# First attention of a fused two-layer kernel: the next batch's projections in two halves, small pieces of TensorE work between the score matmuls, the index load moved to the head of a batch, and the output rows placed in the values' PSUM bank

## The chip, the cores and the metric

The kernel runs on one core of one Trainium2 chip. The metric is the device time of one launch in microseconds (us), lower is better. The core has TensorE (PE, with its weight loads as PEld), VectorE (DVE), ScalarE (ACT), GpSimd (POOL) and SyncE (SP), which run at the same time and wait for each other through semaphores only, and 16 DMA engines, fed by queues of SP, ACT and POOL.

## The reference

Two transformer-like layers over x (16 batches, 128 x 256, float32), cut to what matters:

```python
def _L0_cond_ref(x, mask, Wq, Wo):          # B, D, T = 16, 128, 256; 8 heads of 16
    xt = jnp.transpose(x, (0, 2, 1))
    q = xt @ Wq.T
    qh = q.reshape(B, T, NH, dk).transpose(0, 2, 1, 3)
    scores = scale * jnp.einsum('bhqd,bhkd->bhqk', qh, qh)
    logits = (scores * cmask + (1.0 - cmask) * NEG) * rmask
    attn = jax.nn.softmax(logits, axis=-1)
    ctx = jnp.einsum('bhqk,bhkd->bhqd', attn, qh)
    ...
    out = ctx @ Wo.T
    return jnp.transpose(out, (0, 2, 1))
x = x + _L0_ffn_ref(_L0_cond_ref(x, cond, Wq, Wo), lut, gate_idx, up_idx, down_idx)
x = x + _L1_ffn_ref(_L1_cond_ref(x, cond[:, None, :], ...), ...)
```

`_L0_ffn_ref` is a gated feed-forward net whose weights are entries of a table of 16 values, picked by integer indices (`w = lut[idx]`). `_L1_cond_ref` is a second attention with 16 heads, `_L1_ffn_ref` a mixture of four experts. The change touches the first attention alone, during which the table weights of the first feed-forward net are also built.

## The kernel before, in words

Every engine has a program of its own, written out by hand; its order is the order of the code, and only semaphores (`S["..."]`) tie the engines together. The stages follow one another: the first attention (from some 24 to 298 us of the span), the first feed-forward net, the second attention, the routing, the experts.

The first attention runs over 16 batches. A `body(i, ...)` on each engine works on three of them at once: batch i gets its row maxima, batch i - 1 its softmax and contexts, batch i + 1 its projections. "Batch period" below means the time from one body's first score matmul to the next one's.

The steps of one batch b, with the lines of the profile:

- PE `project` (L764): four matmuls, one for each pair of heads (two instructions each), from the masked x `xm` into PSUM `PA`. The first two fill its first half (512 columns), the last two its second half. ACT `stacks(b, par, h)` (L521, L522) turns half h into bf16 stacks `ks` and `qs`, DVE `lows` (L1170) makes the low parts `low`, and SP `patch` (L313, L317) moves rows of `low` and of the mask into the stacks, by three small DMAs for each half (semaphores `pt0`, `pt1`): one for the mask, behind `ks`, and two of 32 rows of 1 KB behind `lows`.
- PE `scores` (L780) into the two banks of `PB`, one call for each pair c (0 to 3) and row group s (0, 1); it waits for `pt{c // 2}`. DVE `maxima` (L1178) reduces each bank to the row maxima; three short operations (L1185, L1187, L1189) put them into `mcol`, PE `max_rows` (L828) transposes them into `PD`, DVE `add_max` (L1194) adds them into `qs`.
- PE `scores_T` (L792) then makes the transposed scores with the maxima already subtracted, in the two banks of `PC`; it waits for `add_max` (`q2`). ACT `exps` (L536) takes exp of each bank into `probs`.
- PE `project_v` (L772) and ACT `values` (L528) make the values; PE `contexts` (L804) multiplies them with `probs` into `PD[:, 0:512]`, in two calls with `max_rows` of the next batch between; DVE `normalise` in four steps (L1200, L1203, L1206, L1213) divides by the sum; PE `outputs0` (L835) is the output projection; ACT `context_out` (L541) copies it out of PSUM, and POOL `context_parts` (L393, L396) splits it in two bf16 parts. POOL `projected` (L401) masks x two batches ahead.
- Beside it, one chunk c of table weights for each batch (17 chunks, so one is left after the 16 batches): ACT `load_hot` (L550) issues a load of 1 MB of indices (8 rows of 8 KB, each copied to 16 partitions), DVE `one_hot` (L1164) compares, PE `look_up` (L816) multiplies with the table into `PD[:, 512:1024]`, ACT `looked_up` (L546) copies out.

The order around the change is in the `body` functions of PE, ACT and DVE and their calls behind the loop. PE's queue, in order: for each c the calls `scores`, `scores_T` for s = 0 and 1, then a block of other work (`project_v` behind c = 0, the whole `look_up` behind c = 1, `outputs0` and two projections behind c = 2, two projections behind c = 3), then contexts, maxima, contexts. A call of `scores` waits until DVE has reduced the same bank's content from two calls before, a call of `scores_T` until ACT has taken it.

Of the kernel before, what the change touches and what calls it, by code (L numbers as in the profile page):

```python
# [14 lines left out]
P = 128  # L15
B, D, T = 16, 128, 256
# [62 lines left out]
def program(nc, x, cond, condT, consts, wqT, woT, lut, idx_all, w_emb, b_emb, g_norm, w_qkv, g_q, g_k,  # L79
            w_out, w_outT, w_r, b_r, w_all, out, tok_x, tok_r, idx_low, absent_d):  # L80
    with ExitStack() as ctx:
# [420 lines left out]
        def _(act):  # L502
# [13 lines left out]
            def stacks(b, par, h):  # L516
                o = slice(h * 512, (h + 1) * 512)
                act.wait_ge(S["pq"], 2 * b + h + 1)
                if not (isinstance(b, int) and b < 2):
                    act.wait_ge(S["st"], 8 * (b - 1))  # L520
# [17 lines left out]
            def context_out(b):  # L538
                act.wait_ge(S["wo"], b + 1)
                unless_first(act, S["cl"], b)  # L540
                nc.scalar.copy(c_out, PD[:, 512:512 + T]).then_inc(S["c"], 1)  # L541
# [15 lines left out]
            def body(i, par, before=True, after=True):  # L557
                exps(i - 1, 0)
                values(i - 1, 1 - par)
                exps(i - 1, 1)  # L560
                looked_up(i - 1)
                load_hot(i + 1, 1 - par)
                exps(i - 1, 2)
                if before:
                    context_out(i - 2)
                exps(i - 1, 3)
                if after:
                    stacks(i + 1, 1 - par, 0)
# [7 lines left out]
            body(LAST, 1, after=False)  # L576
            exps(LAST, 0)
# [173 lines left out]
        def _(pe):  # L751
# [45 lines left out]
            def contexts(b, par, s):  # L797

                pe.wait_ge(S["vu"], b + 1)
                pe.wait_ge(S["ex"], 8 * b + 8)  # L800
# [8 lines left out]
            def look_up(c, par):  # L809
                pe.wait_ge(S["onehot"], c + 1)  # L810
                pe.wait_ge(S["q2"], min(c + 1, B) if isinstance(c, int) else c + 1)
                if isinstance(c, int) and c >= B:
                    pe.wait_ge(S["c"], LAST)
                bank = PD[:, 512:1024].rearrange("p (h c) -> p h c", h=2)
                for j in range(LPC):
                    ins = mm(bank[:, :, j * LG:(j + 1) * LG], hot[:, par, j * P:(j + 1) * P],  # L816
                             lutw[:].rearrange("p h g -> p (h g)"), start=True, stop=True)
                ins.then_inc(S["lmm"], 1)

            def max_rows(b):  # L820
                pe.wait_ge(S["mc"], 3 * b + 3)
                unless_first(pe, S["w0"], b)
                if not (isinstance(b, int) and b < 2):
                    pe.wait_ge(S["c"], b - 1)
# [6 lines left out]
            def outputs0(b):  # L831
                pe.wait_ge(S["ct"], b + 1)
                pe.wait_ge(S["w0"], LCH if isinstance(b, int) and b == LAST else b + 2)
                for qt in range(KT):
                    ins = mm(PD[:, 512 + qt * P:512 + (qt + 1) * P], cT[:, qt * P:(qt + 1) * P], wo1[:], start=True, stop=True)  # L835
# [12 lines left out]
            def body(i, par, half, before=True, after=True):  # L848
                for c in range(4):
# [3 lines left out]
                    if c == 0:  # L853
                        project_v(i - 1, 1 - par, half)
                    if c == 1:
                        look_up(i - 1, 1 - par)
                    if c == 2 and before:
                        outputs0(i - 2)
                    if c >= 2 and after:
                        project(i + 1, 1 - par, 2 * c - 4)  # L860
# [773 lines left out]
```

## Time and profile before

| | |
|---|---|
| median of 3 runs | 783.81 us (780.01 to 785.44) |
| the profiled execution | 782.84 us, span 781.2 us |
| PE busy in the span | 605.0 us (77%) |
| DVE busy | 430.9 us (55%) |
| ACT busy | 322.0 us (41%) |
| POOL busy | 111.8 us (14%) |
| mean granted clock of TensorE | 0.863 |
| batch 1's first score matmul to batch 15's | 43.75 us to 277.32 us |

The time is that of the launch on the device; the span is the part of it that the profiled instructions fill, 1.6 us less. A busy share is an average over five stages with different limits, so it tells nothing of the stage in question. A granted clock of 1.00 is 2.4 GHz, one of 0.50 is 1.2 GHz; values between are stretches with both. Matmuls overlap in the array, and their ends are modelled, so a busy PE need not be a PE at its peak.

### The profile page before, as it was taken

The numbers are of one execution on the slowest core, as the hardware profiler recorded it, in microseconds if no ns is written. First come the engines' busy times: TensorE is split into PE (matmuls) and PEld (weight loads), VectorE is DVE, ScalarE is ACT, GpSimd is POOL, SyncE is SP. The second block draws the span as 40 slices with busy tenths as digits, with TensorE's granted clock in tenths as the row PEclk, the third lists the DMA queues.
The fourth block names the chain that finished last, engine by engine and source line by source line (L and its number), as shares of the span: only waits on it lengthen the run. The fifth ranks groups of instructions, "written<-read, shape, count | busy, mean of one in ns | idle before, by whom it ended". The sixth has DMA issues, their size and how long they took to land. (4 is left out here: it accounts for less than half of the span.)

```text
span 781.2 us, 15202 instructions
## 1 busy us (share of the span) xinstructions
PE 605.0 (77%) x4891; PEld 375.2 (48%) x4923; DVE 430.9 (55%) x957; ACT 322.0 (41%) x575; POOL 111.8 (14%) x145
## 2 busy tenths in 40 slices
PE   1456788867778869999956787788628999999992
PEld 1134455544455445555533454454414666666662
DVE  2455665675665664334336999999852333333331
ACT  1133454544454543233336777777502222222220
POOL 3401111111111001000000000000011333333321
PEclk9576666786666798999989999999958999999997
DMA  8863333333333320000036566555210111111110
GB/s 281 180 166 79 75 88 96 93 93 76 75 90 87 87 73 2 1 1 0 0 76 179 126 147 146 145 147 137 75 21 28 42 41 40 38 40 43 44 34 3
DMA packets 32739, 62.42 MB, mean 80 GB/s; under 512 B 7109, under 2 KB 19975, under 8 KB 30280
## 3 DMA queue, kind: packets, MB, share of 16 engines
q1 hardware_dynamic: 22112, 23.99, 10.7%
q0 software_dynamic: 6432, 18.46, 10.5%
q10 hardware_dynamic: 4168, 19.61, 9.7%
q8 instruction: 17, 0.28, 0.2%
q14 instruction: 10, 0.08, 0.0%
HBM read 58.81 MB, written 7.82 MB: 85 GB/s over the span
## 5 line engine op out<-in xcount | busy, mean ns | idle before, releaser
L1178 DVE TENSOR_REDUCE nmax<-PB 128x2 f32<-128x512 f32 x128 | 83.7, 677 | 93.8 <-PE PB L780 93.8
L536 ACT ACTIVATE probs<-PC 128x512 f32<-128x512 f32 x128 | 69.5, 595 | 132.2 <-PE PC L792 132.1
L780 PE MATMUL PB<-small 64*128 64x256 bf16 x256 | 46.6, 377 | 69.2 <-DMA small<-small 69.2
L1562 DVE TENSOR_TENSOR probs<-PC,probs 128x1024 bf16<-128x1024 f32 x19 | 23.3, 1225 | 79.9 <-ACT probs L729 65.6
L729 ACT CAST probs<-PC 128x1024 bf16<-128x1024 f32 x19 | 19.2, 1012 | 113.7 <-PE PC L1090 95.6
L764 PE MATMUL PA<-small,wq 128*128 128x256 f32 x128 | 50.6, 534 | 13.9 <-DVE identb L1142 13.9
L1082 PE MATMUL PA<-arena,probs 128*128 x227 | 54.2, 390 | 7.7 <-issue 3.9
L780 PEld LDWEIGHTS PB<-small 64*128 64x128 bf16 x256 | 12.8, 104 | 92.0 <-issue 70.6
L1101 PE MATMUL PD<-arena,probs 128*128 x456 | 53.0, 273 | 2.5 <-issue 2.5
L1082 PE MATMUL PB<-arena,probs 128*128 x210 | 48.6, 379 | 0.9
L1101 PEld LDWEIGHTS PD<-arena,probs 128*128 128x128 bf16 x456 | 44.3, 98 | 8.3 <-issue 3.2
L792 PE MATMUL PC<-small 64*128 64x256 bf16 x256 | 46.4, 376 | 0.9 <-ACT probs L536 0.8
L455 POOL DMA_DIRECT2D arena<-in_w_all x16 | 8.5, 531 | 236.9 <-DVE arena L1416 138.0
L764 PEld LDWEIGHTS PA<-small,wq 128*128 128x128 f32 x128 | 31.1, 270 | 22.8 <-issue 19.0
L661 ACT ACTIVATE probs<-PA,gb 128x1024 f32<-128x1024 f32 x32 | 35.6, 1112 | 15.7 <-PE PA L995 15.7
L1082 PEld LDWEIGHTS PA<-arena,probs 128*128 128x128 bf16 x228 | 22.8, 100 | 35.1 <-issue 15.2
L393 POOL TENSOR_TENSOR arena<-wst,wz 128x256 f32 (+1 forms) x16 | 10.0, 625 | 201.2 <-ACT wst L541 201.2
L804 PE MATMUL PD<-probs,vu 128*32 128x256 f32 x512 | 35.1, 395 | 2.4 <-ACT probs L536 1.4
L1285 DVE TENSOR_TENSOR wst<-PB,wst 128x512 f32<-128x512 f32 (+1 forms) x24 | 16.6, 691 | 36.5 <-PE PB L920 28.2
L477 POOL DMA_INDIRECT out<-probs,tokn x19 | 19.3, 1016 | 116.8 <-DVE probs L1569 116.8
L920 PE MATMUL PB<-arena 128*128 (+1 forms) x143 | 35.8, 386 | 0.1
L920 PE MATMUL PA<-arena 128*128 (+1 forms) x133 | 33.9, 386 | 1.0 <-issue 0.6
(188 smaller groups left out, 1175.5 us busy)
## 6 DMA issues: line engine op xcount, KB each, us to landing
arena<-idx_low ACTq DMA_DIRECT2D x15, 1024.0 KB
wst<-in_w_all SPq DMA_DIRECT2D x48, 256.0 KB, 2.8
arena<-in_w_all POOLq DMA_DIRECT2D x16, 384.0 KB, 6.3
arena<-in_idx_all ACTq DMA_DIRECT2D x1, 2176.0 KB, 11.4
arena<-in_cond SPq DMA_DIRECT2D x16, 128.0 KB, 3.3
small<-in_x SPq DMA_DIRECT2D x16, 128.0 KB, 2.1
small<-small SPq DMA_DIRECT2D x64, 32.0 KB
arena<-idx_low POOLq DMA_DIRECT2D x2, 1024.0 KB, 15.2
```

Of the source, the lines that this page charges most:

```text
L477: pool.indirect_dma_start(out, bass.IndirectOffsetOnAxis(ap=tokn[:, j:j + 1], axis=0), yo[:, j % 2, :], None, bounds_check=TOK - 1, oob_is ...
L536: nc.scalar.activation(probs[:, c, o], PC[:, o], ACT.Exp, scale=SCALE0).then_inc(S["ex"], 1)
L661: nc.scalar.activation(probs[:, 2 * par + c, :], PA[:], ACT.Exp, scale=DK1 ** -0.5, bias=gb[:]).then_inc(S["e3"], 1)
L764: ins = mm(PA[:, pr * T:(pr + 1) * T], wq3[:, pr].rearrange("p a b c -> p (a b c)"), xm[:, par, :], start=True, stop=True)
L780: ins = mm(PB[:, s * 512 + qt * T:s * 512 + (qt + 1) * T], qs[r, par, c * T + qt * P:c * T + (qt + 1) * P], ks[r, par, c * T:(c + 1) * T], ...
L792: ins = mm(PC[:, s * 512 + n * T:s * 512 + (n + 1) * T], ks[r, par, pr * T + kt * P:pr * T + (kt + 1) * P], qs[r, par, pr * T:(pr + 1) * T ...
L804: ins = mm(PD[pr * HS:(pr + 1) * HS, s * T:(s + 1) * T], vu[:, par, kt, 2 * pr + s, :], probs[:, (pr // 2) * KT + kt, o:o + T], start=(kt ...
L920: ins = mm(o, w0(w, which, kt, m), v[:, kt, tok], start=(k == 0), stop=(k == 3 * KT - 1))
L1082: ins = mm(bank[:, n * 512:(n + 1) * 512], v[:, par, xo], w[:, o], start=(k == 0), stop=(k == 3 * KT - 1))
L1101: ins = mm(PD[:, 512:512 + T], v[:, f * P:(f + 1) * P], w[:, o], start=(k == 0), stop=(k == 3 * FT - 1))
L1178: v.tensor_reduce(nmax[:, c, s, :], PB[:, s * 512:(s + 1) * 512].rearrange("p (a k) -> p a k", k=T), AX.X, ALU.max, negate=True).then_inc( ...
L1562: v.tensor_tensor(hT_lo, PC[:], hT_hi, ALU.subtract).then_inc(S["hTl"], 1)
```

## The change

Five things move, and no arithmetic changes:

- PE does one projection of batch i + 1 in each of c = 0, c = 1 (behind s = 0) and two in c = 3 (behind s = 0 and s = 1); `look_up` is cut in two halves of 16 matmuls, and `outputs0` stands behind the last of c = 2.
- ACT's `stacks` for half 0 stands behind `exps(i - 1, 1)`, and its wait asks only for the transposed scores of the same half. DVE's `lows` for half 0 stands behind the reduction (2, 0), that for half 1 ahead of `add_max` and no longer behind it.
- `load_hot(i)` stands at the head of body i; it was `load_hot(i + 1)` after `looked_up`. The load of the last chunk stands behind the last body.
- `outputs0` writes `PD[:, 256:512]`, in the bank of the values and contexts, no longer the bank of the table weights. It waits for the values to be copied out, `max_rows` no longer waits for `context_out`, and the first `contexts` call of a batch now does.

```diff
@@ ACT
             def stacks(b, par, h):
                 act.wait_ge(S["pq"], 2 * b + h + 1)
                 if not (isinstance(b, int) and b < 2):
-                    act.wait_ge(S["st"], 8 * (b - 1))
+                    act.wait_ge(S["st"], 8 * (b - 2) + 4 + 4 * h)
...
-                nc.scalar.copy(c_out, PD[:, 512:512 + T]).then_inc(S["c"], 1)
+                nc.scalar.copy(c_out, PD[:, T:2 * T]).then_inc(S["c"], 1)
...
             def body(i, par, before=True, after=True):
+                if before:
+                    load_hot(i, par)
                 exps(i - 1, 0)
                 values(i - 1, 1 - par)
                 exps(i - 1, 1)
+                if after:
+                    stacks(i + 1, 1 - par, 0)
+                exps(i - 1, 2)
                 looked_up(i - 1)
-                load_hot(i + 1, 1 - par)
-                exps(i - 1, 2)
+                exps(i - 1, 3)
                 if before:
                     context_out(i - 2)
-                exps(i - 1, 3)
                 if after:
-                    stacks(i + 1, 1 - par, 0)
                     stacks(i + 1, 1 - par, 1)
...
             body(LAST, 1, after=False)
+            for c in range(B, LCH):
+                load_hot(c, c % 2)
@@ PE
             def contexts(b, par, s):
                 pe.wait_ge(S["vu"], b + 1)
+                unless_first(pe, S["c"], b)
                 pe.wait_ge(S["ex"], 8 * b + 8)
...
             def max_rows(b):
                 pe.wait_ge(S["mc"], 3 * b + 3)
                 unless_first(pe, S["w0"], b)
-                if not (isinstance(b, int) and b < 2):
-                    pe.wait_ge(S["c"], b - 1)
...
             def outputs0(b):
                 pe.wait_ge(S["ct"], b + 1)
-                pe.wait_ge(S["w0"], LCH if isinstance(b, int) and b == LAST else b + 2)
+                pe.wait_ge(S["vu"], min(b + 2, B) if isinstance(b, int) else b + 2)
...
                         scores_T(i - 1, 1 - par, c, s)
-                    if c == 0:
-                        project_v(i - 1, 1 - par, half)
-                    if c == 1:
-                        look_up(i - 1, 1 - par)
-                    if c == 2 and before:
-                        outputs0(i - 2)
-                    if c >= 2 and after:
-                        project(i + 1, 1 - par, 2 * c - 4)
-                        project(i + 1, 1 - par, 2 * c - 3)
+                        if after and c in (0, 1) and s == 0:
+                            project(i + 1, 1 - par, c)
+                        if (c, s) == (0, 1):
+                            project_v(i - 1, 1 - par, half)
+                        if (c, s) == (1, 1):
+                            look_up(i - 1, 1 - par, 0)
+                        if (c, s) == (2, 0):
+                            look_up(i - 1, 1 - par, 1)
+                        if (c, s) == (2, 1) and before:
+                            outputs0(i - 2)
+                        if after and c == 3:
+                            project(i + 1, 1 - par, 2 + s)
@@ DVE
-            def maxima(b, before=False):
+            def maxima(b, before=False, low_at=None):
...
+                        if low_at is not None and (c, s) == (2, 0):
+                            lows(b + 1, low_at, 0)
...
-                maxima(i, before)
-                if after:
-                    lows(i + 1, 1 - par, 0)
+                maxima(i, before, 1 - par if after else None)
                 one_hot(i, par, half)
-                add_max(i, par)
                 if after:
                     lows(i + 1, 1 - par, 1)
+                add_max(i, par)
```

PE in body 2, from the end of c = 0 to the contexts, before: L764 is a projection of batch 3, L780 and L792 are scores and transposed scores, L816 the whole look-up, L835 the output rows.

```order
L816 MATMUL PD<-lutw,arena 128x2x8 x32
L780 MATMUL PB<-small 128x256 x2
L792 MATMUL PC<-small 128x256 x2
L780 MATMUL PB<-small 128x256 x2
L792 MATMUL PC<-small 128x256 x2
L835 MATMUL PD<-wo,wst 128x128 x2
L764 MATMUL PA<-small,wq 128x256 x2
L780 MATMUL PB<-small 128x256 x2
L792 MATMUL PC<-small 128x256 x2
L780 MATMUL PB<-small 128x256 x2
L792 MATMUL PC<-small 128x256 x2
L764 MATMUL PA<-small,wq 128x256 x2
```

The same stretch of the changed kernel, where L768 is the projection, L784 and L796 the scores and transposed scores, L822 the look-up and L840 the output rows.

```order
L822 MATMUL PD<-lutw,arena 128x2x8 x16
L784 MATMUL PB<-small 128x256 x2
L796 MATMUL PC<-small 128x256 x2
L822 MATMUL PD<-lutw,arena 128x2x8 x16
L784 MATMUL PB<-small 128x256 x2
L796 MATMUL PC<-small 128x256 x2
L840 MATMUL PD<-wo,wst 128x128 x2
L784 MATMUL PB<-small 128x256 x2
L796 MATMUL PC<-small 128x256 x2
L768 MATMUL PA<-small,wq 128x256
L784 MATMUL PB<-small 128x256 x2
L796 MATMUL PC<-small 128x256 x2
```

All four projections stood in the last two steps; now two of them stand in the first two steps, and the look-up is spread over two gaps.

ACT in body 2, from the copy of the look-up (L546) to the end of the body, before: L550 is the index load, L536 the exps, L541 `context_out`, L521 and L522 the stacks.

```order
L546 CAST arena<-PD 128x2x256
L550 DMA arena<-idx_low 128x1x4096
L536 ACTIVATE probs<-PC 128x512 x2
L541 COPY wst<-PD 128x256
L536 ACTIVATE probs<-PC 128x512 x2
L521 ACTIVATE small<-PA,cst 128x512
L522 CAST small<-PA 128x512
L521 ACTIVATE small<-PA,cst 128x512
L522 CAST small<-PA 128x512
```

The same stretch of the changed kernel and the first instructions of the next body (the loop's start, L575, lies between).

```order
L546 CAST arena<-PD 128x2x256
L536 ACTIVATE probs<-PC 128x512 x2
L541 COPY wst<-PD 128x256
L521 ACTIVATE small<-PA,cst 128x512
L522 CAST small<-PA 128x512
L575 UNCONDITIONAL_BRANCH
L575 ISA
L550 DMA arena<-idx_low 128x1x4096
```

The index load stood ahead of four exps and both stacks; it now stands behind all of them.

DVE in body 2 from the last five reductions to its end, before: L1170 is `lows`, L1164 `one_hot`, L1194 `add_max`.

```order
L1178 TENSOR_REDUCE nmax<-PB 128x2 x5
L1185 CAST small<-nmax 128x8x2
L1187 TENSOR_TENSOR small<-nmax,small 128x8x2
L1189 CAST small<-nbig 128x16
L1170 TENSOR_TENSOR small<-PA,small 128x512
L1164 TENSOR_SCALAR arena<-arena,cst 128x4096
L1194 TENSOR_TENSOR small<-PD,small 128x1024
L1170 TENSOR_TENSOR small<-PA,small 128x512
```

The same of the changed kernel, where L1178 is now `lows`, L1186 the reduction, L1172 `one_hot` and L1204 `add_max`.

```order
L1186 TENSOR_REDUCE nmax<-PB 128x2 x2
L1178 TENSOR_TENSOR small<-PA,small 128x512
L1186 TENSOR_REDUCE nmax<-PB 128x2 x3
L1195 CAST small<-nmax 128x8x2
L1197 TENSOR_TENSOR small<-nmax,small 128x8x2
L1199 CAST small<-nbig 128x16
L1172 TENSOR_SCALAR arena<-arena,cst 128x4096
L1178 TENSOR_TENSOR small<-PA,small 128x512
L1204 TENSOR_TENSOR small<-PD,small 128x1024
```

The first half's low part is ready three reductions and a one-hot earlier; `add_max` has become the last operation. SP's and POOL's orders are unchanged.

## Rows read from the trace of the kernel before

**Rows 1.** Engine busy times in the stretch from one batch's first score matmul to the next

```profile
core 0: us, PE busy (x) PEld busy (x) DVE busy (x) ACT busy (x) POOL busy (x), PEclk, DMA share, GB/s
...
160.49:176.80 16.31, 12.22 (x121) 7.90 (x121) 10.70 (x19) 7.77 (x15) 2.01 (x3) 0.73 0.37 91
```

**Rows 2.** Waits of PE from 60 to 280 us: total, times, longest

```profile
PE PB L780 <- DMA small<-small: 52.7, 14, 5.8
```

**Rows 3.** Timeline of the seam between two batches: start, us, engine

```profile
171.81 1.07 PE L804 MATMUL PD<-probs,vu 128*32 128x256 f32 x16
171.85 1.28 DVE L1164 TENSOR_SCALAR arena<-arena,cst 128x4096 bf16<-128x4096 bf16 x1
...
173.05 0.68 DVE L1194 TENSOR_TENSOR small<-PD,small 128x1024 bf16<-128x1024 bf16 x1
...
173.65 0.68 DVE L1170 TENSOR_TENSOR small<-PA,small 128x512 bf16<-128x512 f32 x1
...
174.35 1.21 SPq L317 DMA_DIRECT2D small<-small  x2
...
176.80 0.62 PE L780 MATMUL PB<-small 64*128 64x256 bf16 x3 [3.92 <-DMA small<-small]
```

**Rows 4.** Timeline of the steps c = 2 and 3 of that batch

```profile
164.43 0.78 PE L780 MATMUL PB<-small 64*128 64x256 bf16 x3
...
164.63 0.58 ACT L546 CAST arena<-PD 128x512 f32 x1
164.78 0.64 ACTq L550 DMA_DIRECT2D arena<-idx_low  x1
...
166.78 1.62 PE L764 MATMUL PA<-small,wq 128*128 128x256 f32 x4
...
168.98 1.08 ACT L536 ACTIVATE probs<-PC 128x512 f32<-128x512 f32 x2 [1.58 <-PE PC L792]
169.95 0.69 ACT L521 ACTIVATE small<-PA,cst 128x512 bf16<-128x512 f32 x1
```

**Rows 5.** Timeline: index load, last patches, restart of PE, in two batches

```profile
48.01 1.24 ACTq L550 DMA_DIRECT2D arena<-idx_low  x1
...
55.76 1.12 SPq L317 DMA_DIRECT2D small<-small  x2
60.37 0.81 PE L780 MATMUL PB<-small 64*128 64x256 bf16 x4 [5.85 <-DMA small<-small]
...
115.75 0.65 ACTq L550 DMA_DIRECT2D arena<-idx_low  x1
...
125.88 1.12 SPq L317 DMA_DIRECT2D small<-small  x2
...
127.28 0.62 PE L780 MATMUL PB<-small 64*128 64x256 bf16 x3 [2.96 <-DMA small<-small]
```

**Rows 6.** The page's DMA issues: queue, KB, us from issue to landing

```profile
arena<-in_idx_all ACTq DMA_DIRECT2D x1, 2176.0 KB, 11.4
...
cst<-in_consts SPq DMA_DIRECT2D x1, 215.0 KB, 11.1
```

**Rows 7.** Short stretches, columns as in the first group: the granted clock

```profile
175.00:176.00 1.00, 0.00 (x0) 0.00 (x0) 0.00 (x0) 0.00 (x0) 0.00 (x0) 0.50 0.26 61
...
185.00:186.00 1.00, 1.00 (x10) 0.60 (x10) 0.38 (x1) 0.17 (x1) 0.67 (x1) 0.98 0.43 115
...
440.00:460.00 20.00, 16.12 (x168) 10.00 (x168) 19.03 (x61) 14.97 (x26) 1.06 (x2) 1.00 0.62 146
```

**Rows 8.** Timeline of the last index load and what waits for it

```profile
281.62 0.65 ACTq L550 DMA_DIRECT2D arena<-idx_low  x1
...
283.92 1.09 ACT L536 ACTIVATE probs<-PC 128x512 f32<-128x512 f32 x2 [0.20 <-PE PC L792]
...
293.13 1.29 DVE L1164 TENSOR_SCALAR arena<-arena,cst 128x4096 bf16<-128x4096 bf16 x1 [3.34 <-DMA arena<-idx_low]
...
295.42 3.02 PE L804 MATMUL PD<-probs,vu 128*32 128x256 f32 x32
```

More of the change, by code:

```diff
@@ L807, in contexts, with look_up @@
                     ins.then_inc(S["ctx"], 1)
[L809 to L813, printed above, removed]
+            def look_up(c, par, part_=None):
+                if part_ != 1:
+                    pe.wait_ge(S["onehot"], c + 1)
+                    pe.wait_ge(S["q2"], min(c + 1, B) if isinstance(c, int) else c + 1)
+                    if isinstance(c, int) and c >= B:
+                        pe.wait_ge(S["w0"], c)
                 bank = PD[:, 512:1024].rearrange("p (h c) -> p h c", h=2)
-                for j in range(LPC):
+                for j in range(*{None: (0, LPC), 0: (0, LPC // 2), 1: (LPC // 2, LPC)}[part_]):
                     ins = mm(bank[:, :, j * LG:(j + 1) * LG], hot[:, par, j * P:(j + 1) * P],
                              lutw[:].rearrange("p h g -> p (h g)"), start=True, stop=True)
-                ins.then_inc(S["lmm"], 1)
+                if part_ != 0:
+                    ins.then_inc(S["lmm"], 1)
             def max_rows(b):
@@ L832, in outputs0 @@
                 pe.wait_ge(S["ct"], b + 1)
-                pe.wait_ge(S["w0"], LCH if isinstance(b, int) and b == LAST else b + 2)
+                pe.wait_ge(S["vu"], min(b + 2, B) if isinstance(b, int) else b + 2)
                 for qt in range(KT):
-                    ins = mm(PD[:, 512 + qt * P:512 + (qt + 1) * P], cT[:, qt * P:(qt + 1) * P], wo1[:], start=True, stop=True)
+                    ins = mm(PD[:, T + qt * P:T + (qt + 1) * P], cT[:, qt * P:(qt + 1) * P], wo1[:], start=True, stop=True)
                 ins.then_inc(S["wo"], 1)
```

## The prediction

> **What bounds the kernel now.** I read the stretches by batch first. From batch 1 to batch 15 a period is (277.32 - 43.75) / 14 = 16.68 us, and in the one shown no engine fills it: DVE is busy 10.7 us, ACT 7.8, PE 12.2, at a mean clock of 0.73 [rows 1]. So the limit is a chain with a wait in it. The waits name it: PE stood before a batch's first scores for the patch DMAs, 14 times, 52.7 us in all, 3.8 us a batch [rows 2]. At the seam [rows 3] PE ends its contexts at 172.88; DVE does `one_hot`, `add_max` and only then `lows` for half 1, until 174.33; SP issues the last two patches at 174.35; PE starts again at 176.80. So far this reads as a chain through the low parts, which the change shortens by some 5 us.
>
> The next view speaks of another chain. From the last patches' issue to PE's restart it takes 4.6 us in one batch, 1.4 in another [rows 5] and 2.5 in the third [rows 3]. From the index load's issue to the same restart it is 12.4, 11.5 [rows 5] and 12.0 us [rows 3, 4]; over all 14 batches 11.5 to 12.7, mean 12.1, whereas the first distance runs from 1.4 to 4.6, long where the patches came early after the load and short where they came late. In the batch of 4.6 us they were issued 7.8 us behind the load, in that of 1.4 us 10.1 us behind it. A load alone lands 11.5 us after its issue (281.62 to 293.13) [rows 8]. The reader is to see that small patches which find the load under way land when it is over, however early they were issued. The start of the kernel has it too: the constants, a tenth of the bytes, issued on SP's queue right behind the big index list on ACT's, took 11.1 us where the list took 11.4 [rows 6].
>
> The wait also costs clock: 0.50 from 175 on, back only at 185 [rows 7], so the scores after a stop of 4 us start at 1.2 GHz.
>
> **Part by part.** *What the halves gain.* Half 0's patches now leave DVE three reductions, `one_hot` (1.28), a second `lows` and `add_max` ahead of the seam, and no load has just started then: the stop at the first scores goes, 3.8 us a batch.
>
> *What the load's new place costs.* ACT issues `load_hot(k)` right behind the second half of `stacks(k)`. Half 1's patches of the same batch k come after it: `lows` of half 1 needs those stacks, stands behind `one_hot` on DVE, and SP issues two DMAs behind that. So each batch's half 1 patches are issued some 2 us after a load of 1 MB, where before at least 7.8 us lay between [rows 5]. PE needs them at `scores` (2, 0). If they land with the load, that is 11.8 us after its issue: 11.5 from the load alone, 12.1 from the mean of the 14 batches, in which both halves' patches were held; now half as many are. The ends are 11.4 and 12.4.
>
> *The rest of the loop*, from `scores` (2, 0) to the next `load_hot` on ACT. Before, from the same call (164.43) to the end of the last exp (170.06) it took 5.6 us, at the lower clock except for the end [rows 4]. It loses one pair's worth of projection ahead of that exp (1.62 / 2 for one of the two, 0.8) and gains half a look-up, 0.5: 5.3. It stays at the lower clock throughout, since PE has stood for 6 us: some 0.5 more. `lows` of half 0 in DVE's reductions costs 0.6 if `scores` (3, 1) waits for it, which I put at 0.1, DVE having caught up. Then `context_out` (0.37), the first stack (0.6 to 0.7) and the load's issue 0.15 us after the second begins, as 164.78 is behind 164.63 [rows 4]: 1.1. Sum 7.0 us. With a clock that is back early it is 6.2, with more weight changes showing 8.0.
>
> *Period:* 11.8 + 7.0 = 18.8 us, between 17.6 and 20.4. Against 16.68 this is 14 x 2.1 = 29.7 us lost. PE stands from the middle of step c = 1 for about 6 us in every batch, and queued behind it are both scores, the look-up's second half, and through them DVE's reductions and ACT's exps. Against this loop DVE's 10.7 us and everything else is covered.
>
> *The end.* The last load was issued 3.4 us before the end of body 15's last exp (285.01). It now goes out 0.15 us behind that, lands 11.5 us later, then `one_hot` 1.3 and the look-up 1.0, and PE's last contexts stand behind it: 14.0 us after the exp, where it was 10.4 (295.42) [rows 8]. 3.6 us lost; nothing hides them, since the feed-forward net needs these contexts.
>
> *At nothing:* `contexts` waits 0.4 us for `context_out`, and `max_rows`, the next scores and `add_max` are queued behind it, but all of these end before the held patches do. If no patch is held, it still ends at 11.2 us of an 11.5 us period. The smaller pieces of PE's work, the output rows' new bank and `max_rows` without its wait fill gaps that the loop covers.
>
> **Sum.** 782.84 + 29.7 + 3.6 = **816 us**. The median of the runs lies 1 us above this execution; about 1% (8 us) is what a measurement of this kernel can tell from no change.
>
> The rule of the Trainium skill that bears on this (DMA: Bandwidth & Descriptors, Queues, rings and completion order) is that each DMA engine goes round the queues that have work but finishes a whole packet, typically 9 to 17 descriptors, before it switches. By that rule the trace agrees: the load's 128 rows of 8 KB on few engines would be a packet or two on each. The same page (Issuing engines are not separate DMA queues) says that transfers of different engines interleave; taken to mean that small ones slip in between, it would give the sum of the first rival.
>
> **Rivals.** *The patches slip in between, and it gets much faster.* The place is the DMA engines just after the load's start, the price the whole 11.8 us. DVE then sets the pace: 10.7 us busy [rows 1], 0.6 for `lows` waiting for the stacks of half 0, 0.2 for collisions, and 0.9 for a clock that falls now and then and a load that `one_hot` meets late: P = 12.4, and 782.84 - 14 x 4.3 + 3.6 = 727 us. It decides from a landing of 16.4 - 7.0 = 9.4 us after the load's issue: earlier is a gain, since at P = 16.4 the 3.6 us of the end are just paid. For it: the clock of the second attention is 1.00 with PE busy 16.1 of 20 us in pieces [rows 7], so nothing else would hold it back. Against it: with it the batch of 4.6 us would have been one of 2 to 3.
>
> *Half a load.* If the engines switch once in the middle of the load, the patches land at about 8 us: P = 8.0 + 6.5 = 14.5, 756 us. Against it: two patches are needed, and the second would fall behind the load's other half.
>
> *A wash.* The landing at 9.4 to 10 and the clock back early give P near 16.4: 779 to 789 us. No row is near it.
>
> *Worse.* If the fall of the clock also stretches steps c = 0 and 1 until the stacks come later, or the x and mask loads of SP sit in front of the patches, P = 20.5 and more: 840 us. Against it: they are issued a step later.
>
> *The change doesn't do what it says*, half 0's stop staying: its patches are issued about when the previous load ends, 11.8 us after its issue, and the first scores follow 4 us later. I see no row for it.
>
> **How the numbers follow.** Forecast (P 17.4 to 20.2; 796 to 836 us) 0.75; slips in between (715 to 742) 0.12; half a load (743 to 770) 0.07; a wash 0.04; worse 0.02. The forecast's own range is 796 to 836. The range that holds 8 in 10 has to reach into the second rival: it leaves out the first, 0.12, a third of the half load, 0.03, and the worst end: 752 to 834. Slower by over 1%: 0.77; within 1%: 0.04; faster: 0.19.
>
> **What would show it.** In the profile of the changed kernel PE's wait for the small DMAs should still be there, longer (some 5.5 to 6 us, 14 times, 80 us), but in the middle of a batch, at `scores` (2, 0), and not before the first scores. From a load's issue to PE's restart it should again be 11.4 to 12.4 us. The clock should be about 0.7 as before. The last contexts should start some 14 us after the end of body 15's last exp. Wrong it is if no wait of scores for a DMA stands at c = 2, or if it ends well before 11 us after the load's issue; then DVE is near its 10.7 us in a period of 12 to 13, and the clock above 0.9.

## The result and the profile after

The changed kernel takes 840.35 us (median of 4 runs, 839.60 to 841.69), the kernel before 781.91 (779.96 to 785.44) beside it: a ratio of 1.074, interval 1.070 to 1.079. It is slower by 58 us, 6 us beyond the top of the range that was to hold 8 in 10 (834) and 4 us beyond that of the forecast itself (836).

The page of the changed kernel, its span, busy times and the granted clock in 40 slices of 21 us:

```profile
span 839.2 us, 15233 instructions
...
PE 670.5 (80%) x4922; PEld 389.6 (46%) x4923; DVE 433.4 (52%) x957; ACT 327.2 (39%) x575; POOL 125.3 (15%) x145
...
PEclk9996666666666776799999799999975999999997
```

DVE and ACT are busy about as long as before (430.9 and 322.0 us), and PE loads its weights as often (4923 times). But PE's busy time is up by 65 us with the same work. The lower clock alone doesn't explain that: over the first attention its mean is 0.72 (24 to 350 us), where it was 0.71 (24 to 295 us). The larger part is the cut itself. Before, both row groups of a step c followed each other, eight small matmuls in a row, here from 168.34 to 168.89, when the projection starts (L780 scores, L792 transposed scores, L784 and L796 in the changed kernel):

```profile
168.34 0.40 PE L780 MATMUL PB<-small 64*128 64x256 bf16 x4
168.57 0.39 PE L792 MATMUL PC<-small 64*128 64x256 bf16 x4
168.89 1.13 PE L764 MATMUL PA<-small,wq 128*128 128x256 f32 x4
```

In the changed kernel other work stands between the row groups, and four of these matmuls take as long as the eight did, here from 162.62 to 163.16, when the projection starts:

```profile
162.62 0.39 PE L784 MATMUL PB<-small 64*128 64x256 bf16 x2
162.85 0.38 PE L796 MATMUL PC<-small 64*128 64x256 bf16 x2
```

So eight took 0.55 us and four 0.54 at full clock; at the lower one it is 0.98 (before, 162.49 to 163.47) and 0.96 (after, 170.84 to 171.80). Matmuls of the two row groups overlap when they are neighbours, and the cut parts them four times a batch. With two steps of a batch at either clock that is 2 x 0.54 + 2 x 0.96 = 3.0 us of PE a batch, some 45 us in 15 batches, an estimate. The rest of the 65 us goes to the clock, as far as the rows show: in the batch shown below some 11 us of PE's work run at the lower one, in that of [rows 1] 6.4. The prediction had the smaller pieces at nothing.

The waits from 60 to 280 us (engine, line, releaser: total, times, longest), which answers to [rows 2]:

```profile
PE PB L784 <- DMA small<-small: 38.3, 11, 3.9
```

Still once a batch, 3.5 us for 3.8 in the mean, but a batch is now longer, and the stop is elsewhere in it. The timeline of one batch, which answers to [rows 3 to 5] (L550 the index load, L317 the patches, L784 scores, L768 projections, L840 the output rows, L536 exps):

```profile
158.80 0.64 ACTq L550 DMA_DIRECT2D arena<-idx_low  x1
...
160.25 1.11 SPq L317 DMA_DIRECT2D small<-small  x2
...
162.62 0.39 PE L784 MATMUL PB<-small 64*128 64x256 bf16 x2
...
163.16 0.70 PE L768 MATMUL PA<-small,wq 128*128 128x256 f32 x2
...
170.84 0.60 PE L784 MATMUL PB<-small 64*128 64x256 bf16 x2 [3.60 <-DMA small<-small]
...
173.29 1.22 PE L840 MATMUL PD<-wo,wst 128*128 128x128 f32 x4
...
175.40 1.22 PE L768 MATMUL PA<-small,wq 128*128 128x256 f32 x2
...
177.62 0.60 ACT L536 ACTIVATE probs<-PC 128x512 f32<-128x512 f32 x1 [1.52 <-PE PC L796]
...
178.91 0.64 ACTq L550 DMA_DIRECT2D arena<-idx_low  x1
```

The batch's first scores (162.62) wait for nothing: half 0's stop is gone. The stop stands at `scores` (2, 0). From the load's issue to the restart it is 12.04 us, from there to the next load 8.07 us, together the period: (320.01 - 77.16) / 12 = 20.24 us from the issue of batch 3's load to that of batch 15's. Over all batches the first stretch is 11.7 to 12.6 us, mean 12.1 (14 stops), the second 7.9 to 8.5, mean 8.2 (13, without the last batch). The two stretches by engine (columns as in [rows 1]):

```profile
158.80:170.84 12.04, 8.44 (x81) 4.46 (x73) 6.03 (x11) 4.51 (x9) 2.26 (x3) 0.78 0.50 115
170.84:178.91 8.07, 8.07 (x44) 4.31 (x48) 4.32 (x9) 3.26 (x7) 0.22 (x1) 0.50 0.02 8
```

In the first the DMA engines move 115 GB/s and PE stands at the end of it. In the second hardly anything moves (8 GB/s), and PE is busy all of the time at a clock of 0.50. The load is over before these 8 us of work begin, so they hide nothing of it.

The end, which answers to [rows 8]:

```profile
336.76 0.64 ACTq L550 DMA_DIRECT2D arena<-idx_low  x1
337.13 0.59 ACT L536 ACTIVATE probs<-PC 128x512 f32<-128x512 f32 x1
...
347.78 1.29 DVE L1172 TENSOR_SCALAR arena<-arena,cst 128x4096 bf16<-128x4096 bf16 x1 [2.91 <-DMA arena<-idx_low]
...
350.01 3.55 PE L809 MATMUL PD<-probs,vu 128*32 128x256 f32 x32
```

The last contexts start 12.3 us after the end of the last exp of body 15 (337.72), where it was 10.4.

So the 58.0 us between the spans are: batch 1's first scores 1.0 us earlier; 14 periods of (323.65 - 42.74) / 14 = 20.06 against 16.68, 47.3; body 15 from its first scores to that exp 14.1 against 7.7, 6.4, since half 1 of batch 15 is held too; the end 1.9; and from the start of the last contexts to the end of the span 489.2 against 485.8, 3.4.

### The profile page after: what moved, and what is told of

Read it like the earlier page. It is cut to its first block and busy times, and to the rows that moved or that the text cites. A ratio compares the mean times of both kernels' runs of the same rounds, so it can differ in the third digit from the quotient of the medians.

```text
span 839.2 us, 15233 instructions
## 1 busy us (share of the span) xinstructions
PE 670.5 (80%) x4922; PEld 389.6 (46%) x4923; DVE 433.4 (52%) x957; ACT 327.2 (39%) x575; POOL 125.3 (15%) x145
## 5 line engine op out<-in xcount | busy, mean ns | idle before, releaser
L1186 DVE TENSOR_REDUCE nmax<-PB 128x2 f32<-128x512 f32 x128 | 87.3, 686 | 121.7 <-PE PB L784 120.1
L536 ACT ACTIVATE probs<-PC 128x512 f32<-128x512 f32 x128 | 75.8, 598 | 185.9 <-PE PC L796 185.3
L784 PE MATMUL PB<-small 64*128 64x256 bf16 x256 | 61.7, 346 | 67.0 <-DMA small<-small 66.9
L768 PE MATMUL PA<-small,wq 128*128 128x256 f32 x128 | 63.4, 595 | 13.8 <-DVE identb L1150 13.8
L796 PE MATMUL PC<-small 64*128 64x256 bf16 x256 | 62.2, 344 | 0.9 <-ACT probs L536 0.8
L784 PEld LDWEIGHTS PB<-small 64*128 64x128 bf16 x256 | 14.8, 101 | 103.4 <-issue 80.6
L393 POOL TENSOR_TENSOR arena<-wst,wz 128x256 f32 (+1 forms) x16 | 22.8, 1422 | 257.4 <-ACT wst L541 257.4
L809 PE MATMUL PD<-probs,vu 128*32 128x256 f32 x512 | 55.2, 577 | 1.5 <-ACT wst L541 1.5
L1090 PE MATMUL PB<-arena,probs 128*128 x228 | 52.3, 379 | 0.0
L768 PEld LDWEIGHTS PA<-small,wq 128*128 128x128 f32 x128 | 27.2, 261 | 33.4 <-issue 32.9
L1090 PEld LDWEIGHTS PA<-arena,probs 128*128 128x128 bf16 x228 | 22.5, 99 | 34.7 <-issue 14.5
L976 PE MATMUL PB<-wqkv,small 128*128 128x512 f32 x64 | 34.0, 657 | 2.1 <-ACT small L636 2.1
```

The costliest lines, as they stand in the source:

```text
L536: nc.scalar.activation(probs[:, c, o], PC[:, o], ACT.Exp, scale=SCALE0).then_inc(S["ex"], 1)
L768: ins = mm(PA[:, pr * T:(pr + 1) * T], wq3[:, pr].rearrange("p a b c -> p (a b c)"), xm[:, par, :], start=True, stop=True)
L784: ins = mm(PB[:, s * 512 + qt * T:s * 512 + (qt + 1) * T], qs[r, par, c * T + qt * P:c * T + (qt + 1) * P], ks[r, par, c * T:(c + 1) * T], ...
L796: ins = mm(PC[:, s * 512 + n * T:s * 512 + (n + 1) * T], ks[r, par, pr * T + kt * P:pr * T + (kt + 1) * P], qs[r, par, pr * T:(pr + 1) * T ...
L809: ins = mm(PD[pr * HS:(pr + 1) * HS, s * T:(s + 1) * T], vu[:, par, kt, 2 * pr + s, :], probs[:, (pr // 2) * KT + kt, o:o + T], start=(kt ...
L976: ins = mm(PB[:, 0:512], xnT[:, kt, :], wqkv[:, kt, 0:512], start=(kt == 0), stop=(kt == KT - 1))
```

## The experiments

Each ratio is against the kernel before on the same chip.

**Small loads, in both kernels.** `[:, par, 0:LHOT // 16]` on both sides of the load: it moves a sixteenth of the indices, and the rest of a chunk's table weights are made from what the buffer held.

```diff
-                act.dma_start(hot[:, par, :], hot_rows(c)).then_inc(S[f"hot{par}"], 16)
+                act.dma_start(hot[:, par, 0:LHOT // 16], hot_rows(c)[:, :, 0:LHOT // 16]).then_inc(S[f"hot{par}"], 16)
```

The changed kernel with it. 

> The changed kernel with each of the 15 index loads of the loop cut to a sixteenth of its columns (64 KB, not 1 MB; the rest of the chunk's indices is not loaded, so the table weights are wrong, the same instructions run). Theory, half 1's patches are held by the load issued 2 us before them: the wait at scores (2, 0) goes, the period falls from 20.2 us to 12 to 13 us, the clock goes above 0.9, and the time to 720 to 735 us. Rival, the small pieces of TensorE work and the low clock set the pace: the period stays above 18 us, 820 us and more. Rival, the patches are late by themselves (DVE and SP reach them late): the wait shrinks by under 1 us, 825 us or more.

Measured: 727.85 us (726.73 to 728.51), ratio 0.928 [0.923, 0.933]. No scores wait for a DMA, the clock is 1.00 from 130 to 180 us with PE busy 47.98 of 50 us, and a period is (216.90 - 57.59) / 13 = 12.25 us, as expected. So the load's bytes are the cause of 8.0 us a batch, with what they cost in clock; nothing else of the change stands in the way of a 12.3 us period. PE is full in it (DVE is busy 42.56 of the 50 us).

The kernel before with it. 

> The kernel before with the same cut of the loads to a sixteenth. Theory, the wait at the seam was bound by the load too, but only by its last part: the restart comes 1.4 to 1.6 us after the last patches' issue in every batch, so the period falls by some 0.8 us and the time to 768 to 774 us. Rival, the seam was a pure chain through the low parts: 780 to 784 us. If e1 gains over 100 us and this one about 10, the halves' gain is real and hidden by the load.

Measured: 738.37 us in the median of four runs (726.15, 738.32, 738.42 and 740.18), some 30 us lower than expected. From 60 to 280 us:

```profile
PE PB L780 <- DMA small<-small: 20.4, 13, 1.7
```

Its timeline shows what a free patch takes: issued at 105.44, restart at 107.90, so 2.46 us; under a load it is 10.6 (160.25 to 170.84 above). The period is (232.47 - 43.86) / 14 = 13.47 us, so the load cost the kernel before 3.2 us a batch, more than my expectation had left to it. This trace is of the run of 738.42 us, at a clock of 0.84 from 130 to 180 us. Between the medians of the two small-load kernels 10.5 us remain, but the fastest run here, 726.15, is no slower than the changed kernel's fastest, 726.73. So with the load out of the way the other parts of the change bring between nothing and 10.5 us. Perhaps the stop which they remove and the overlap which they give up cancel in that run; there is no trace of it.

**The load back in its old place, the rest of the change kept.** In ACT's `body` (the load behind the last body goes too):

```diff
-                if before:
-                    load_hot(i, par)
                 exps(i - 1, 0)
...
                 looked_up(i - 1)
+                load_hot(i + 1, 1 - par)
                 exps(i - 1, 3)
```

> The changed kernel with the load of the next chunk back behind the copy of the look-up (in the middle of the body), all else as changed. Theory: the load is then issued some 4 us behind the restart at scores (2, 0) and still holds half 1's patches until 12 us after its issue, so the period is 12 + 3.7 = 15.7 us and the time 770 to 785 us. Rival, only the nearness of load and patches matters (2 us apart in the changed kernel, 4 us here): no wait at c = 2, a period of 12 to 13 us, 730 us. Rival, the pieces cost the time: above 820 us.

Measured: 807.97 us (804.19 to 810.19), ratio 1.028 [1.023, 1.034]. So the halves with the old place lose too, 24 us against the 783.80 us beside it. It is 23 us above the expectation, and the patches that are held are not half 1's at `scores` (2, 0) but half 0's, at the next batch's first scores. The timeline shows two kinds of batch in turn:

```profile
142.37 0.64 ACTq L550 DMA_DIRECT2D arena<-idx_low  x1
142.55 1.44 SPq L317 DMA_DIRECT2D small<-small  x2
...
152.82 0.60 PE L781 MATMUL PB<-small 64*128 64x256 bf16 x2 [4.64 <-DMA small<-small]
162.73 1.14 SPq L317 DMA_DIRECT2D small<-small  x2
163.47 0.64 ACTq L550 DMA_DIRECT2D arena<-idx_low  x1
```

Half 0's patches, which the change makes earlier, meet the load's issue. Where they are 0.2 us behind it (142.55) they land 10.45 us after it; where they are 0.7 us ahead (162.73) nobody waits. Less than one microsecond of order decides on a stop of 5 us. The stop comes in every second batch (6 times from 60 to 280 us).

**The load at the head, all else as before** (and the last one behind the last body).

```diff
+                if before:
+                    load_hot(i, par)
                 exps(i - 1, 0)
                 values(i - 1, 1 - par)
                 exps(i - 1, 1)
                 looked_up(i - 1)
-                load_hot(i + 1, 1 - par)
```

> The kernel before with one part of the change alone, the load at the head of the body it serves (and the last one behind the last body). Theory: the last patches, still issued at the seam, follow the load by 2.5 us and are held: half 1's patches land 12 us after the load and scores (2, 0) waits for them, the period is 12 + 7.2 = 19.2 us, 822 us; if half 0's patches are held too, PE starts the batch 12 us after the load and the period is 23 us, 875 us. Rival, the load's place is harmless alone: 780 to 790 us.

Measured: 859.43 us (856.60 to 868.54), ratio 1.093 [1.088, 1.099].

```profile
97.76 0.67 ACTq L550 DMA_DIRECT2D arena<-idx_low  x1
...
101.66 1.11 SPq L317 DMA_DIRECT2D small<-small  x2
...
109.78 0.62 PE L783 MATMUL PB<-small 64*128 64x256 bf16 x3 [9.65 <-DMA small<-small]
```

Both halves' patches are behind the load here, and the first scores wait 9.7 us, to 12.0 us after its issue. It is the second branch of the expectation: a period of 23 us was expected for it, and (323.23 - 75.20) / 11 = 22.5 came; its 875 us were 859 in the median, 868.54 in the run of this trace. The load's new place alone costs 76 us; the rest of the change gives 19 of them back.

**Two loads of half the size in the changed kernel.** Each chunk is cut in two column halves of 512 KB. The first half of chunk i goes out behind the first exp of body i, the second half of chunk i + 1 behind the body's last exp; in the last body both go out behind `looked_up`, so nothing is left for the end.

```diff
+            def load_half(c, par, n):
+                o = slice(n * (LHOT // 2), (n + 1) * (LHOT // 2))
+                act.dma_start(hot[:, par, o], hot_rows(c)[:, :, o]).then_inc(S[f"hot{par}"], 16)
...
+                    if s == 0 and mid is not None:
+                        load_half(mid, par, 0)
...
-                if before:
-                    load_hot(i, par)
-                exps(i - 1, 0)
+                exps(i - 1, 0, i if before else None, par)
...
                 looked_up(i - 1)
+                if not after:
+                    load_half(i + 1, 1 - par, 0)
+                    load_half(i + 1, 1 - par, 1)
                 exps(i - 1, 3)
+                if after:
+                    load_half(i + 1, 1 - par, 1)
@@ DVE
-                    dve.wait_ge(S[f"hot{par}"], 16 * half)
+                    dve.wait_ge(S[f"hot{par}"], 32 * half)
```

> The changed kernel with each index load cut into two column halves (512 KB each): the first half of chunk i issued behind the first exponential of half 0 of body i, the second half of chunk i+1 behind the last one of half 0 of the body before. Theory (patches issued behind a load land when the load does, so what counts is how many bytes are under way when a row of patches is issued): a half load takes some 5 to 6 us, lies under the exponentials, and no first scores wait longer than 1 to 2 us for patches; the period of a batch falls from 20.24 us to the 12.3 us of the kernel with small loads, and the time is 722 to 745 us. Rival (each load under way costs its place a full wait, whatever its size): two held halves a batch, over 840 us. Rival (half loads still hold the patches in part and the clock falls): 760 to 800 us.

Measured: 731.28 us (729.69 to 733.82), ratio 0.937 [0.933, 0.941], the fastest kernel that computes everything, 3.4 us above the one with small loads. Timeline of one batch:

```profile
157.24 0.64 ACTq L553 DMA_DIRECT2D arena<-idx_low  x1
...
160.17 1.11 SPq L317 DMA_DIRECT2D small<-small  x2
...
161.92 0.64 ACTq L553 DMA_DIRECT2D arena<-idx_low  x1
...
165.69 0.39 PE L788 MATMUL PB<-small 64*128 64x256 bf16 x2
...
169.86 0.64 ACTq L553 DMA_DIRECT2D arena<-idx_low  x1
```

and the stretch of four batches around it:

```profile
130.00:180.00 50.00, 46.42 (x479) 27.00 (x478) 42.06 (x76) 31.25 (x61) 10.57 (x12) 1.00 0.46 115
```

Half 1's patches are issued 2.9 us behind a half load (160.17 behind 157.24) and `scores` (2, 0) use them at 165.69 with no wait. The same bytes, 115 GB/s over the stretch, are hidden, and none of the places has a whole megabyte in front of patches. The period is 12.62 us (157.24 to 169.86), and the clock stays at 1.00.

**The same two half loads in the kernel before**, the second one behind `looked_up`. 

> The kernel before with its loads cut into two column halves: the first half of chunk i behind the first exponential of body i, the second half of chunk i+1 behind the look-up. Theory: patches are no longer held; what is left is the batch of the kernel before with a load of no price, as it stood with small loads (726 to 740 us): 730 to 750 us. Set beside the changed kernel with two half loads it tells what the split heads are worth alone; expected is at most 1.2 us a batch (20 us in all).

Measured: 740.65 us (735.63 to 745.71), ratio 0.947 [0.942, 0.951]. From 60 to 280 us, besides other rows:

```profile
PE PB L785 <- DMA small<-small: 20.9, 13, 1.7
```

That is the 1.6 us stop of a free patch. It is what the split heads remove. The clock is 0.75 from 130 to 180 us here and 1.00 in the changed kernel with half loads. Yet all parts of the change together are worth 9.4 us, 0.6 us a batch, once the load is out of the way: less than the stop itself. The parted row groups probably take some of it back (2.2 us of PE a batch at full clock, 4 x 0.54), but no run changed the pieces alone.

**The load at the head in four pieces** of 256 KB, one issued behind the other (DVE waits for all four).

```diff
-                act.dma_start(hot[:, par, :], hot_rows(c)).then_inc(S[f"hot{par}"], 16)
+                for n in range(4):
+                    o = slice(n * (LHOT // 4), (n + 1) * (LHOT // 4))
+                    act.dma_start(hot[:, par, o], hot_rows(c)[:, :, o]).then_inc(S[f"hot{par}"], 16)
```

> The changed kernel with the load at the head of a batch issued as four column pieces of 256 KB, one behind the other on ScalarE's queue. If transfers of different queues take turns, and a patch waits only for the piece under way, half 1's patches land some 7 us after the first piece's issue, the wait of first scores for DMA is gone, and the time is 735 to 770 us. If what was issued first moves first, whatever it is cut into, the patches still land about 12 us after the first issue, the period stays at about 20 us, and ScalarE's three further issues (0.64 us each) add up to 1 us a batch: 835 to 860 us.

Measured: 794.08 us (786.48 to 797.95), ratio 1.015 [1.008, 1.022], between the two expectations.

```profile
161.00 0.64 ACTq L552 DMA_DIRECT2D arena<-idx_low  x1
161.81 2.21 ACTq L552 DMA_DIRECT2D arena<-idx_low  x3
162.78 1.43 SPq L317 DMA_DIRECT2D small<-small  x2
171.06 0.60 PE L786 MATMUL PB<-small 64*128 64x256 bf16 x2 [1.81 <-DMA small<-small]
...
213.29 0.64 ACTq L552 DMA_DIRECT2D arena<-idx_low  x1
214.09 2.24 ACTq L552 DMA_DIRECT2D arena<-idx_low  x3
214.66 1.11 SPq L317 DMA_DIRECT2D small<-small  x2
221.71 0.60 PE L786 MATMUL PB<-small 64*128 64x256 bf16 x2 [0.90 <-DMA small<-small]
```

The patches land 10.1 and 8.4 us after the first piece, not 12.0: with pieces they do pass some of the backlog. At 3 us a piece (12 us by four) and 2.5 us for a free patch, two to two and a half pieces still go first, an estimate. A period is (264.37 - 91.05) / 10 = 17.3 us.

The rule of the Trainium skill named in the prediction (DMA: Bandwidth & Descriptors, Queues, rings and completion order: a whole packet is finished before an engine turns to another queue) would allow both, but these runs don't show a packet.

**The whole load 3 us later**, behind half 1's patches.

```diff
-                if before:
-                    load_hot(i, par)
                 exps(i - 1, 0)
+                if before:
+                    load_hot(i, par)
```

> The changed kernel with the whole load of 1 MB moved behind the last exponential of half 0 of the same body, about 3 us later, behind the issue of half 1's patches. Theory: half 1's patches are in front of the load and are not held; half 0's patches of the next body are issued some 5 us behind the load and land 11 to 12 us after it, so its first scores wait about 2 us, and the one-hot rows come late: a period of 14 to 15.5 us, 750 to 775 us. Rival (the load costs the same wherever it lies): a period near 20 us, 820 to 840 us.

Measured: 802.55 us (801.89 to 803.07), ratio 1.027 [1.022, 1.033]: 28 us above the expectation.

```profile
170.18 0.64 ACTq L550 DMA_DIRECT2D arena<-idx_low  x1
...
174.89 1.12 SPq L317 DMA_DIRECT2D small<-small  x2
...
182.26 1.28 DVE L1172 TENSOR_SCALAR arena<-arena,cst 128x4096 bf16<-128x4096 bf16 x1 [4.40 <-DMA arena<-idx_low]
...
182.97 0.39 PE L784 MATMUL PB<-small 64*128 64x256 bf16 x2 [2.41 <-DMA small<-small]
...
184.87 0.60 PE L796 MATMUL PC<-small 64*128 64x256 bf16 x2 [1.52 <-DVE small L1204]
```

The waits have the sizes that were expected: patches issued 4.7 us behind the load end with it (2.4 us of waiting), and the one-hot rows wait for the load itself, which takes 12.1 us. But this happens in every second batch only (6 such waits of the scores from 60 to 280 us), and the period is (222.74 - 116.31) / 6 = 17.7 us and not 15. I had left out the clock: behind each such stop a stretch runs at the lower clock, 0.60 us for two matmuls of the scores or transposed scores (184.87) that take 0.38 to 0.39 at the full one. The batch behind the stop is then so long that its load seems to be in time; that this alternation is the clock's doing is read from the timeline and not tested.

**Is it the clock?** Twenty-four matmuls of no use ahead of the wait at `scores` (2, 0) in the changed kernel (shown), 56 of 128x128 ahead of the first scores' in the kernel before.

```diff
+                if fill and (c, s) == (2, 0):
+                    for n in range(24):
+                        mm(PB[:, n % 2 * T:(n % 2 + 1) * T], qs[r, par, n % 2 * P:n % 2 * P + P], ks[r, par, 0:T],
+                           start=True, stop=True)
                 pe.wait_ge(S[f"pt{c // 2}"], 48 * b + 48)
```

> The changed kernel with 24 matmuls more, of no use, that TensorE issues ahead of its wait at the first scores of half 1 (0.195 us each at full clock, 4.7 us of a wait that a full clock would make 5.1 us long); the load and its place stay. Theory (patches land 12.0 us after the load is issued, and what closes the loop is the way from the restart to the next issue, 8.07 us of it at the lower clock, 5.3 to 5.7 us in the kernel with two half loads at full clock): with TensorE kept busy the granted clock stays up, the period falls from 20.24 to about 17.6 us, and the time is 800 to 812 us. Rival (the clock falls all the same, or the way back isn't bound by TensorE's speed): 835 to 845 us.

Measured: 830.90 us (826.10 to 839.83), ratio 1.066 [1.059, 1.074], between the two expectations.

```profile
161.64 2.79 PE L784 MATMUL PB<-small 64*128 64x256 bf16 x24
165.00 0.39 PE L788 MATMUL PB<-small 64*128 64x256 bf16 x2 [0.57 <-DMA small<-small]
...
167.33 0.60 PE L788 MATMUL PB<-small 64*128 64x256 bf16 x2
...
171.80 0.64 ACTq L550 DMA_DIRECT2D arena<-idx_low  x1
```

The 24 matmuls took 2.79 us and not the 4.7 expected, so TensorE still stands for 0.57 us here, and for 0.4 to 2.4 in the other batches in which it waits. It now restarts at full clock (0.39), but the clock falls 2.3 us later all the same (0.60 at 167.33). The way back to the load is 6.80 us here, 7.6 in the mean of the six batches that the next figure spans, for 8.2; the period is (230.98 - 113.39) / 6 = 19.60 for 20.24. With the load's 12.0 us untouched, the period falls by what the way back falls, 0.6 us. That this is 9 us of the whole fits the medians (9.5), but the four runs lie between 826.10 and 839.83, so the times alone would not show it. So the loop is right. But the matmuls take away only about a quarter of what the clock costs there.

> The kernel before with 56 matmuls more of 128x128, of no use, ahead of its wait at the first scores of a batch (some 3.5 us of a wait of 3.8 us). Theory: the clock stays up behind the wait, the wait itself stays or grows, since it ends with the load; the way from the restart to the next load is shorter by 1 to 2 us a batch: 750 to 772 us. Rival (the batch is bound by what the load and ScalarE take, not by the clock): 778 to 786 us. Worse (the added matmuls outlast the wait where it is short): 785 to 800 us.

Measured: 774.50 us (770.98 to 775.86), ratio 0.989 [0.985, 0.993]: a small gain of the same kind, between the two expectations. The period is (225.06 - 80.33) / 9 = 16.08 us for 16.68. The clock is 0.88 from 60 to 280 us, where it was 0.70, and the scores still restart 11.8 to 12.6 us after the load's issue: while a transfer ends the wait, clock buys only what it takes off the way back.

## Why the prediction was right and wrong

*Right: the mechanism.* "Small patches which find the load under way land when it is over" gave the direction against what the change seems to do, and the small-load kernel tests it: 727.85 us, where the prediction had 727 if the patches slip in between, at a period of 12.25 for the 12.4 forecast. That they agree so closely is partly luck: the 12.4 was built on DVE's pace, and in the run it is PE that is full. The half-load rival and the wash were ruled out by the landing of 12.0 us.

*Right: what the halves gain.* Half 0's stop is gone, in every batch.

*The load's new place:* 11.8 us forecast, 12.04 measured in the batch shown, 12.1 in the mean, with 11.4 to 12.4 as bounds; one of the 14 lies above them (12.6).

*The step that failed: the rest of the loop*, 7.0 us forecast with 8.0 as the upper end, 8.07 measured in the batch shown and 8.2 in the mean. From the restart to the end of the last exp it is 7.38 us (170.84 to 178.22), where 5.9 was forecast; the 1.1 us behind the exp were 0.7. Two terms were too small.

The first is the clock. The prediction reads the 5.6 us of [rows 4] as "at the lower clock except for the end" and adds 0.5 for a lower clock throughout. The reading is right, but the end is long:

```profile
167.00:168.00 1.00, 1.00 (x3) 0.80 (x3) 0.00 (x0) 0.37 (x1) 0.40 (x1) 0.51 0.50 164
168.00:169.00 1.00, 1.00 (x11) 0.45 (x10) 0.24 (x1) 0.02 (x1) 0.81 (x2) 1.00 0.47 123
```

From 168 on, so for 2.1 of the 5.6 us, the clock was full. The changed kernel with two half loads runs the same instructions at full clock in 4.63 us (165.69 to 170.32), so the lower clock makes such a stretch 1.6 times as long. For 2.1 us that is about 1.2 us and not 0.5, an estimate.

The second is the cut, which stands under *At nothing*: "The smaller pieces of PE's work" were to "fill gaps that the loop covers". The loop does cover those of c = 0 and 1. But in c = 2 and 3 they lie on the way back to the load. In c = 2, at the lower clock in both kernels, the scores took 1.34 us before (164.43 to 165.77) and take 2 x 0.96 after: 0.6 us more. The two terms make 1.3 of the 1.5 us between 5.9 and 7.38. No run separates them.

*A second term at nothing: body 15.* The sum has 14 periods, up to body 15's first scores, and the end, from its last exp. What lies between was 7.7 us and is 14.1, since the stop of body 15 comes behind its first scores. These 6.4 us are in no term.

*The count.* The period came out at 20.06 in the mean, inside the forecast's own 17.6 to 20.4. With it and the 3.6 us of the end the sum would have been 833.7. The rest is body 15, 6.4 us; 3.4 us behind the attention, which I can't explain (the runs of the kernel before lie 5 us apart); less 1.0 at the start and 1.7 at the end. So the longer loop used up the range, and body 15 took the time out of it.

*The end:* 3.6 us forecast, 1.9 measured. The load goes out 0.96 us ahead of the end of that exp and not behind it, and lands in 11.0 us.

*The wait's length:* 5.5 to 6 us forecast, 3.6 measured, at no cost. The contexts ran at the lower clock, and the parted row groups of c = 0 and 1 take longer, so TensorE arrived later at the same landing. A wait that a transfer ends is no measure of its price.

*The rivals.* The time is that of "worse", 840 us, but not its mechanism: steps c = 0 and 1 run at full clock (0.70 at 163.16), and nothing of SP's stands in front of the patches.

## What to carry to other kernels

Where a large load and small transfers that an engine waits for share the DMA engines, look at which is issued first, to the microsecond, and at how long the small one would take alone: here 2.5 us alone, 10.6 behind 1 MB. Cutting the load in two and giving each half a place where no small transfer follows closely was worth 40 us in the kernel before and 109 in the changed one; moved as a whole, at any of three places in the changed kernel, it never beat the kernel before. To size a stretch that follows a stop, find first at which clock its model in the trace ran, by one instruction whose duration is known at both. And before work is put between two instructions, look whether the trace has them overlap: here a step's eight small matmuls took no longer than four of them alone.

## What was not expected of the hardware

Keeping TensorE busy through most of its wait did not keep the clock at full: in the changed kernel it fell 2.3 us behind the restart (0.39 to 0.60 us for two score matmuls), though PE had stood for only 0.57 us. From 60 to 280 us it rose from 0.67 to 0.78. Which activity before it decided is open.

A load cut into four pieces on one queue lets transfers of another queue pass in part: landing 8.4 to 10.1 us after the first piece against 12.0.

In the changed kernel the matmuls fill 46.4 of 50 us at full clock once no load is in the way, 11.7 of the 12.6 us of a batch. At a clock of 0.50 they would not fit into it, an estimate.

Parting neighbouring matmuls of the two row groups doubles what they take, at either clock (0.55 us for eight, 0.54 for four; 0.98 and 0.96).
